# Masked attention stage: score matmuls in four 32-row tiles, one PSUM bank for three uses, and a new order within each batch

## The chip, the cores and the metric

The kernel runs on one NeuronCore of a Trainium2 chip. The metric is the device time of one execution in microseconds (us). The engines are TensorE (PE in the profile, its weight loads PEld), VectorE (DVE), ScalarE (ACT), GpSimd (POOL) and SyncE (SP), each with an instruction stream of its own; they meet at semaphores only. Matmuls write PSUM, which has eight banks of 128 x 512 fp32; VectorE and ScalarE read PSUM, GpSimd reads SBUF only.

## The reference

Four transformer blocks follow one another on `x` (16 batches x 128 rows x 256), each attending to itself or to a context. The change lies in the third block alone, here "the masked stage":

```python
# L2, per layer: self attention with ltor_mask, then cross attention with cross_mask; 16 heads of 16
def attention(q, k, v, mask):
    scores = einsum('bhqd,bhkd->bhqk', q, k) / sqrt(16)
    scores = scores * mask - 10000.0 * (1.0 - mask)
    probs = softmax(scores, axis=-1)
    return einsum('bhqk,bhkd->bhqd', probs, v)
ln_out = layernorm(x); q, k, v = split(ln_out @ w_qkv + b_qkv)          # layer 0
x = x + merge_heads(attention(q, k, v, ltor_mask)) @ w_ao + b_ao
q = layernorm(x) @ w_q + b_q; k, v = split(context @ w_kv + b_kv)        # layer 1
x = x + merge_heads(attention(q, k, v, cross_mask)) @ w_co + b_co
```

Both layers run over 16 batches of 128 queries and 128 keys, so the stage handles 32 batches of one layer each.

## The kernel before

**A window per batch.** `over_sequence` (L397) calls each engine's `window(n, at)` for n = -4 to 34; window n is the one in which batch n of the 32 has its scores ("core"). In the same window `soon` is batch n+1, `ahead` n+2, `past` n-1, `tail` n-2, `late` n-3. Windows 0 to 8 and most others are written out; 9, 10 and 19 to 26 are the bodies of loops. A window has four steps j, one for four heads each (g = 4n + j numbers them). The order of each engine's instructions is the order of the source; nothing is planned at run time. SyncE only loads context rows and masks for this stage.

**A batch's path.** VectorE normalizes the rows (`normalize`, L2295), TensorE turns them and the context rows into `in_bank` (L1349, L1353), ScalarE copies them out scaled as `rows_t` and `cn_t` (L1780, L1791). TensorE projects queries and keys into `project2_bank` (L1376, L1318) and values into `rows_bank` (L1367). VectorE adds the bias to queries and keys (`qk`, L2347) and to values (`vn`, L2329). GpSimd spreads the keys (`spread`, L2766): for one half of the channels (8 heads of 16 rows) it writes `km`, four copies of the keys side by side, each multiplied by a column of 0 and 1 (`head_in_half`) that keeps one head of four.

**Scores.** A head's 16 rows can't be addressed alone, so a matmul contracts 64 rows (four heads) with the spread keys, 4 x 128 columns, and the zeros keep the heads apart. At j = 0 and j = 2 two such matmuls go to the upper and the lower 64 rows of the array and to banks 0 and 1:

```python
for r in range(2):
    half = slice(r * P // 2, (r + 1) * P // 2)
    pe.matmul(score_bank[r][:, :], qk[u][half, j // 2, :], km[u][half, j // 2, :], start=True, stop=True)
```

**Softmax and result.** For each step VectorE multiplies the bank by the mask (L2322), GpSimd adds the mask's bias (L2786), VectorE takes the negative maximum of each head (L2334), ScalarE the exponentials (four instructions, L1752), TensorE turns the four heads' probabilities (`turn_bank`, L1302), ScalarE copies them (L1758), TensorE sums values (L1336, four tiles of 32 columns, one for each head). Once a batch's four sums are done ScalarE copies them (L1762), TensorE turns them back (`unturned_bank`, L1359), VectorE divides by the row sums (L2354, L2094: "heads taken"), TensorE turns the heads (L1309), ScalarE copies them (L1767), TensorE multiplies by the output weights (`rows_bank`, L1325) and VectorE adds to `x` (L2314).

**VectorE's other work.** In each even window at j = 1: one normalization (L2300) and the mean and variance of two later batches (`measure`, `shift`, L2284 to L2292); in each odd window a normalization at j = 3. In windows 0 to 7 also, at j = 1, `standardized` (L2258): two instructions (L2263, L2267) that finish a row of the stage before.

**Banks.** 0 and 1 scores, 2 turned probabilities, 3 sums, 4 projections of queries and keys, 5 turned inputs, 6 sums turned back, 7 in two halves, `rows_bank` and `heads_bank`.

Of the kernel before, what the change touches and what calls it, by code (L numbers as in the profile page):

```python
# [20 lines left out]
F32 = mybir.dt.float32  # L21
# [3 lines left out]
ACT = mybir.ActivationFunctionType  # L25
X_AXIS = mybir.AxisListType.X

P = 128
B = 16
D = 256  # L30
# [462 lines left out]
def program(nc, t, out, outer):  # L493
# [7 lines left out]
    bank = [outer.enter_context(nc.psum_tensor(f"bank{k}", [P, BANK], F32)) for k in range(8)]  # L501
# [56 lines left out]
    with ExitStack() as scope1:  # L558
        head_of_16 = sbuf(scope1, "head_of_16", [P, HN // 2])
        head_in_half = sbuf(scope1, "head_in_half", [P, PACK])  # L560
        vn = [sbuf(scope1, f"vn{u}", [P, UNITS, HN, QUAD]) for u in range(SLOTS)]
# [242 lines left out]
    def _(pe):  # L804
# [473 lines left out]
        def layer2():  # L1278
# [4 lines left out]
            def window(n, at, u=None):  # L1283
                u = n % SLOTS if u is None else u
                core, past, tail, late = at(0), at(-1), at(-2), at(-3)
                soon, ahead = at(1), at(2)
                for j in range(STEPS):
                    g = STEPS * n + j
                    if core and j % 2 == 0:

                        pe.wait_ge(s.spread, 2 * n + j // 2 + 1)
                        after(pe, s.masked, g)
                        for r in range(2):
                            half = slice(r * P // 2, (r + 1) * P // 2)
                            pe.matmul(score_bank[r][:, :], qk[u][half, j // 2, :], km[u][half, j // 2, :], start=True, stop=True)\
                              .then_inc(s.scores, 1)
                    if core and j == 3 or past and j < 3:
                        pe.wait_ge(s.exp_ready, g - 2)
                        after(pe, s.probs_copied, g - 3)
                        t = (j - 3) % STEPS  # L1300
                        for m in range(PACK):
                            last = pe.transpose(turn_bank[:, m * P:(m + 1) * P], probs[t][:, m * P:(m + 1) * P], ident[:, :])  # L1302
                        last.then_inc(s.probs_turned, 1)
                    if late and j == 1:
                        pe.wait_ge(s.heads_taken, n - 2)
                        if core:
                            pe.wait_ge(s.v_ready, n + 1)
                        for c in range(DC):
                            last = pe.transpose(heads_bank[:, c * P:(c + 1) * P], heads_out[0][:, c * P:(c + 1) * P], ident[:, :])  # L1309
                        last.then_inc(s.heads_turned, 1)  # L1310
                    if soon and j == 1:
                        layer, b = soon
                        keys_of = cn_t[1 - u] if layer else rows_t[1 - u]
                        if layer:
                            pe.wait_ge(s.context_ready, b + 1)
                        for m in range(DC, 2 * DC):
                            for c in range(DC):
                                last = pe.matmul(project2_bank[:, m * P:(m + 1) * P], w_qkv[:, layer, c, m * P:(m + 1) * P],  # L1318
                                                 keys_of[:, c, :], start=c == 0, stop=c == DC - 1)
                        last.then_inc(s.projected, 1)  # L1320
                    if late and j == 2:
                        layer = late[0]
                        pe.wait_ge(s.heads_copied, n - 2)
# [4 lines left out]
                        if isinstance(n, int) and n == 2 * B + 1:  # L1328
                            turn_hidden(ROUNDS)
                    for t in (0, 1) if past and j == 1 else (j,) if past and j else ():  # L1330
                        pe.wait_ge(s.probs_copied, g - j + t - 3)
                        if t == 0:
                            pe.wait_ge(s.v_ready, n)
                            after(pe, s.sums_copied, n - 1)
                        for m in range(PACK):
                            last = pe.matmul(sums2_bank[m * QUAD:(m + 1) * QUAD, t * P:(t + 1) * P], vn[1 - u][:, 0, PACK * t + m, :],  # L1336
                                             probs_t[t][:, m * P:(m + 1) * P], start=True, stop=True)
                        last.then_inc(s.sums, 1)
                    if ahead and j == 0:

                        layer, b = ahead
                        if isinstance(n, int) and n == -2:
                            unread(19, sums2_bank)
                        pe.wait_ge(s.rows_normed, n + 3)
                        after(pe, s.in_ready, n + 2)
                        if layer:
                            after(pe, s.context_ready, b)
                        for c in range(DC):
                            last = pe.transpose(in_bank[:, c * P:(c + 1) * P], norm_rows[:, u, c * P:(c + 1) * P], ident[:, :])  # L1349
# [1618 lines left out]
```

## Time and profile before

| | |
|---|---|
| median of 3 runs | 2274.27 us (2271.91 to 2277.16) |
| the profiled execution | 2272.06 us, its span 2270.3 us |
| mean granted TensorE clock | 0.992 |
| masked stage, first scores to the last addition | 1468.8 to 1835.1 us |
| busy in the whole span | PE 2179.0 us (96%), PEld 1779.6, ACT 1573.0 (69%), DVE 1554.7 (68%), POOL 725.4 (32%) |

A busy share is no limit by itself: matmuls are pipelined, so that an engine that is busy nearly all the time may yet wait for operands. What matters for the change is how long one window of the masked stage lasts, and which instruction waits for which in it.

### The profile page before, as it was taken

The page shows a single profiled execution, that of the slowest core. Times are in us where ns is not written, and L with a number is a line of the kernel's source. Part 1 is how long each engine was busy: PE and PEld are TensorE (multiplying, and loading weights), DVE is VectorE, ACT ScalarE, POOL GpSimd, SP SyncE. Part 2 cuts the span into 40 slices and gives each one's busy share as a digit, 9 for nine tenths or more (in the row PEclk, how much of TensorE's full clock was granted, in tenths as well). Part 3 has the DMA queues.
Part 4 walks back from the last instruction along what each step waited for, and adds up shares of the span by engine and source line. Part 5 has one row for each costly group of instructions (what it writes and reads, how often), then busy time and mean ns, then how long its engine had stood idle before and what let it go on. Part 6 is the DMA issues. An engine that isn't in the chain of part 4 may idle for free. (4 is left out here: it accounts for less than half of the span.)

```text
span 2270.3 us, 51859 instructions
## 1 busy us (share of the span) xinstructions
PE 2179.0 (96%) x17621; PEld 1779.6 (78%) x17621; DVE 1554.7 (68%) x3940; ACT 1573.0 (69%) x4479; POOL 725.4 (32%) x885
## 2 busy tenths in 40 slices
PE   8999999999999999998999999889999989999998
PEld 7899999998999999997985666556666679766664
DVE  6555555567555555557759999687776676899985
ACT  4666666665667666665737777577788776578875
POOL 2211111123211111102124655377777720233201
PEclk9999999999999999999989999999999999999999
DMA  5100112010010000002000000100000000000001
GB/s 135 24 25 24 24 25 61 24 24 1 24 24 25 24 24 24 1 1 64 11 8 11 11 9 6 39 8 2 6 15 17 14 8 5 7 11 11 7 4 38
DMA packets 72945, 47.16 MB, mean 21 GB/s; under 512 B 29232, under 2 KB 71600, under 8 KB 72752
## 3 DMA queue, kind: packets, MB, share of 16 engines
q1 hardware_dynamic: 70576, 43.57, 7.3%
q8 instruction: 117, 1.92, 0.3%
q10 hardware_dynamic: 2176, 1.05, 0.2%
q14 instruction: 76, 0.62, 0.1%
HBM read 41.45 MB, written 2.10 MB: 19 GB/s over the span
## 5 line engine op out<-in xcount | busy, mean ns | idle before, releaser
L2155 DVE TENSOR_REDUCE maxima<-bank 128x2 f32<-128x512 f32 x512 | 332.6, 681 | 30.4 <-PE bank L1103 28.3
L1715 ACT ACTIVATE probs_t<-bank 128x512 f32<-128x512 f32 x512 | 282.4, 601 | 64.8 <-PE bank L1092 63.4
L2011 DVE SCALAR_TENSOR_TENSOR wide_heads_low<-bank,wide_columns,wide_heads_high 128x128 fp32r<-128x128 f32 x512 | 155.8, 346 | 209.3 <-ACT wide_heads_high L1580 209.2
L1568 ACT ACTIVATE wide_probs<-bank,wide_neg_max 128x129 f32<-128x129 f32 x512 | 184.2, 365 | 118.7 <-DVE wide_neg_max L1991 114.4
L1563 ACT ACTIVATE wide_probs_t<-bank 128x256 f32<-128x256 f32 x256 | 98.3, 384 | 161.7 <-PE bank L959 159.5
L2512 POOL TENSOR_TENSOR wide_columns<-wide_pair_columns,zero 128x8 f32<-128x8 f32 x16 | 3.3, 209 | 640.7 <-DVE x L2024 638.9
L1995 DVE RECIPROCAL wide_inverse<-wide_sums 128x2 f32<-128x2 f32 x256 | 42.4, 166 | 227.7 <-ACT wide_probs L1568 227.7
L1574 ACT ACTIVATE wide_probs<-wide_probs,wide_inverse 128x128 f32<-128x128 f32 x448 | 156.1, 396 | 52.0 <-DVE wide_inverse L1995 52.0
L1092 PE MATMUL bank<-q_packed,k_packed 32*128 32x256 f32 x1024 | 167.6, 330 | 7.5 <-ACT probs_t L1715 6.8
L1103 PE MATMUL bank<-k_packed,q_packed 32*128 32x256 f32 x1024 | 172.6, 334 | 2.2 <-DVE maxima L2155 1.1
L1752 ACT ACTIVATE probs<-scores_masked,neg_max 128x128 f32<-128x128 f32 x512 | 163.2, 394 | 10.7 <-DVE neg_max L2334 10.0
L973 PEld LDWEIGHTS bank<-wide_probs_t,wide_v 128*128 128x128 f32 x1024 | 148.0, 190 | 26.3 <-ACT wide_probs_t L1563 10.0
L807 PE MATMUL bank<-wide_weights_high,wide_heads_high 128*128 128x256 f32 x512 | 165.6, 323 | 0.2 <-DVE wide_heads_low L2011 0.2
L1092 PEld LDWEIGHTS bank<-q_packed,k_packed 32*128 32x128 f32 x1024 | 104.0, 185 | 74.1 <-ACT probs_t L1715 37.0
L973 PE MATMUL bank<-wide_probs_t,wide_v 128*128 128x128 f32 x1024 | 157.1, 276 | 4.7 <-ACT wide_probs_t L1563 4.7
L946 PE MATMUL bank<-wide_k,wide_q 128*128 128x129 f32 x1024 | 156.0, 275 | 3.0 <-POOL wide_normed_low L2538 1.5
L1580 ACT ACTIVATE wide_heads_high<-bank,wide_columns 128x128 fp32r<-128x128 f32 x512 | 155.2, 353 | 1.5 <-PE bank L973 0.8
L807 PE MATMUL bank<-wide_weights_high,wide_ctx_high 128*128 128x256 f32 x512 | 148.2, 289 | 0.0
L946 PEld LDWEIGHTS bank<-wide_k,wide_q 128*128 128x128 f32 x1024 | 139.9, 190 | 9.6 <-POOL wide_normed_low L2538 2.2
L809 PE MATMUL bank<-wide_weights_high,wide_heads_low 128*128 128x256 f32 x512 | 143.9, 281 | 0.0
L808 PE MATMUL bank<-wide_weights_low,wide_heads_high 128*128 128x256 f32 x512 | 143.9, 281 | 0.0
L808 PE MATMUL bank<-wide_weights_low,wide_ctx_high 128*128 128x256 f32 x512 | 142.9, 279 | 0.0
(319 smaller groups left out, 6799.5 us busy)
## 6 DMA issues: line engine op xcount, KB each, us to landing
cn<-in_ctx SPq DMA_DIRECT2D x48, 128.0 KB, 2.1
q_packed<-max_rows SPq DMA_DIRECT2D x256, 4.0 KB
wide_pair_weights<-in_L_xattn_wq SPq DMA_DIRECT2D x15, 256.0 KB, 2.7
wide_pair_weights<-in_L_xattn_wk SPq DMA_DIRECT2D x15, 256.0 KB, 3.2
wide_pair_weights<-in_L_xattn_wv SPq DMA_DIRECT2D x15, 256.0 KB, 3.5
wide_pair_weights<-in_L_xattn_wo SPq DMA_DIRECT2D x15, 256.0 KB, 3.3
x<-in_x SPq DMA_DIRECT2D x4, 512.0 KB, 7.1
wide_ctx_rows<-in_ctx SPq DMA_DIRECT2D x4, 512.0 KB, 8.7
```

The costliest lines, as they stand in the source:

```text
L807: pe.matmul(acc, wh, mh, start=start, stop=False)
L808: pe.matmul(acc, wh, ml, start=False, stop=False)
L946: last = pe.matmul(wide_scores[b % 2][:, h * KEYS0:(h + 1) * KEYS0], q0[k % 2][:, h, b * P:(b + 1) * P], k0[k % 2][:, h, b, :], start=True ...
L973: last = pe.matmul(wide_heads[a % 2][:, h * P:(h + 1) * P], v0[parity][:, a, h * P:(h + 1) * P], probs_t0[:, a, h, :], start=True, stop=True)
L1092: last = pe.matmul(shifted_bank[j % 2][:, c * D:(c + 1) * D], k_packed[u][quad[a], pack, c * P:(c + 1) * P], q_packed[u][quad[a], pack, :] ...
L1103: last = pe.matmul(head_scores[packed_scores(1 - u, j)][:, c * D:(c + 1) * D], q_packed[1 - u][quad[b], pack, c * P:(c + 1) * P], k_packed ...
L1568: last = act.activation(probs0[:, b, h, :], wide_scores[b % 2][:, h * KEYS0:(h + 1) * KEYS0], ACT.Exp, bias=neg_max0[:, b, h:h + 1], accum ...
L1574: last = act.activation(probs0[:, b, h, 0:P], probs0[:, b, h, 0:P], ACT.Copy, scale=inverse0[:, b, h:h + 1])
L1715: act.activation(probs_t[j % 8][:, :], shifted_bank[j % 2][:, :], ACT.Exp, bias=0.0).then_inc(s.exp_ready, 1)
L1752: last = act.activation(probs[t][:, part], scores_masked[t][:, part], ACT.Exp, bias=neg_max[t][:, h:h + 1])
L2011: last = dve.scalar_tensor_tensor(heads_low[:, h, a, :], wide_heads[a % 2][:, h * P:(h + 1) * P], columns[slot][:, 3, h:h + 1], heads_high ...
L2155: dve.tensor_reduce(maxima[pack // 2][:, b, pack % 2, :], head_scores[packed_scores(1 - u, j)][:, :].rearrange("p (a k) -> p a k", a=UNITS ...
```

## The change

- **Scores.** Four matmuls for each of j = 0 and 2, each on 32 rows of the array (two heads), with 2 x 128 columns of spread keys, into four banks (0 to 3, 256 columns of each). The semaphore is raised after the second and the fourth.
- **Spread keys.** GpSimd writes two copies in place of four: `head_in_quad`, two columns, for `head_in_half`.
- **Mask product** (L2322): reads two half-filled banks in one instruction in place of a full one.
- **Banks.** Turned probabilities go to bank 4, sums to 5; inputs turned, projections, and sums turned back share bank 6, one after the other. The rows and heads bank 7 gets more waits (`heads_copied` ahead of the values and of `vn`).
- **Order.** Inputs of a batch are turned in the window before its scores, no longer two before, and queries and keys are projected together at j = 2. TensorE's window is now (before, the steps j = 0 to 3 were: scores, turn, inputs | turn, heads, keys, two sums, sums back | scores, turn, result, sum | turn, sum, values, queries):

```text
j = 0   scores 0, 1 | turn probs 1 of past | turn inputs of soon
j = 1   result of late | turn probs 2 | sums 0, 1 | sums turned back of tail
j = 2   scores 2, 3 | turn probs 3 | project queries and keys of soon
j = 3   turn probs 0 of core | values of soon | heads of tail | sums 2, 3
```

VectorE adds the bias to queries and keys at j = 3, after the mask product; it takes the heads at j = 2, after the mask product and the maxima of that step, and adds the result to `x` behind them. ScalarE copies the inputs all at j = 0 and the heads at j = 3.

```diff
-    score_bank = [bank[0], bank[1]]
-    turn_bank = bank[2]
-    sums2_bank = bank[3]
-    project2_bank = bank[4]
-    in_bank = bank[5]
-    unturned_bank = bank[6]
+    score_banks = banks[:, 0:PACK, 0:D]
+    turn_bank = bank[4]
+    sums2_bank = bank[5]
+    project2_bank = in_bank = unturned_bank = bank[6]
...
@@ TensorE, window
-                        for r in range(2):
-                            half = slice(r * P // 2, (r + 1) * P // 2)
-                            pe.matmul(score_bank[r][:, :], qk[u][half, j // 2, :], km[u][half, j // 2, :], start=True, stop=True)\
-                              .then_inc(s.scores, 1)
+                        for a in range(PACK):
+                            last = pe.matmul(score_banks[:, a, :], qk[u][quad[a], j // 2, :], km[u][quad[a], j // 2, 0:2 * P], start=True, stop=True)
+                            if a % 2:
+                                last.then_inc(s.scores, 1)
...
+                    if late and j == 1:
+                        layer = late[0]
+                        pe.wait_ge(s.heads_copied, n - 2)
                         if core:
                             pe.wait_ge(s.v_ready, n + 1)
...                                                  # result of late: into rows_bank
+                    if past and j == 1:
+                        turn_probs(g, j)
+                        sum_pair(n, g, j, u)
                     if tail and j == 1:
                         pe.wait_ge(s.sums_copied, n - 1)
                         after(pe, s.heads_taken, n - 2)
+                        if soon:
+                            pe.wait_ge(s.in_ready, n + 2)
+                            if soon[0]:
+                                pe.wait_ge(s.context_ready, soon[1] + 1)
+                        elif core:
+                            pe.wait_ge(s.qk_ready, n + 1)
...                                                  # sums turned back of tail
+                    if soon and j == 2:
+                        layer, b = soon
+                        keys_of = cn_t[1 - u] if layer else rows_t[1 - u]
+                        pe.wait_ge(s.in_ready, n + 2)
+                        if layer:
+                            pe.wait_ge(s.context_ready, b + 1)
+                        if tail:
+                            pe.wait_ge(s.heads_taken, n - 1)
+                        for m in range(2 * DC):
+                            rows = rows_t[1 - u] if m < DC else keys_of
+                            for c in range(DC):
+                                last = pe.matmul(project2_bank[:, m * P:(m + 1) * P], w_qkv[:, layer, c, m * P:(m + 1) * P],
+                                                 rows[:, c, :], start=c == 0, stop=c == DC - 1)
+                        last.then_inc(s.projected, 1)
...
+            def turn_probs(g, j):
+                pe.wait_ge(s.exp_ready, g - 2)
+                after(pe, s.probs_copied, g - 3)
...
+            def sum_pair(n, g, j, u):
+                for t in (0, 1) if j == 1 else (2, 3):
+                    pe.wait_ge(s.probs_copied, g - j + t - 3)
...
@@ VectorE, window
+                        pair = slice(2 * (j % 2), 2 * (j % 2) + 2)
+                        dve.tensor_tensor(scores_masked[j][:, :].rearrange("p (a h k) -> p a h k", a=2, h=2),
+                                          score_banks[:, pair, :].rearrange("p a (h k) -> p a h k", h=2),
+                                          mask[:, 0:1, :].unsqueeze(2).broadcast_to([P, 2, 2, P]), ALU.mult).then_inc(s.masked, 1)
...
+                    if soon and j == 3:
+                        layer = soon[0]
+                        dve.wait_ge(s.projected, n + 2)
...                                                  # qk; then the maxima of the step before
-                    if tail and j == 3:
+                    if tail and j == 2:              # behind the mask product and the maxima of j = 2
                         dve.wait_ge(s.sums_turned, n - 1)
                         after(dve, s.heads_turned, n - 2)
...
@@ GpSimd, spread
-                    pool.tensor_tensor(km[slot][:, c, :].rearrange("p (h k) -> p h k", h=PACK),
-                                       qk[slot][:, DC + c:DC + c + 1, :].broadcast_to(wide),
-                                       head_in_half[:, :].unsqueeze(2).broadcast_to(wide), ALU.mult).then_inc(s.spread, 1)
+                    pool.tensor_tensor(km[slot][:, c, 0:2 * P].rearrange("p (h k) -> p h k", h=2),
+                                       qk[slot][:, DC + c:DC + c + 1, :].broadcast_to(twice),
+                                       head_in_quad.unsqueeze(2).broadcast_to(twice), ALU.mult).then_inc(s.spread, 1)
```

## Rows read from the trace of the kernel before

**Rows 1.** Windows 8, 9: PE, PEld, DVE, ACT, POOL busy; clock, DMA

```profile
1558.66:1580.83 22.17, 21.05 (x177) 14.28 (x177) 16.08 (x33) 17.00 (x49) 16.32 (x16) 1.00 0.01 2
```

**Rows 2.** The score matmuls alone in stretches of whole windows, eight records a window

```profile
1468.80:1490.88 22.08, 5.46 (x16) 1.44 (x16) 0.94 0.00 1
1490.88:1558.66 67.78, 13.55 (x49) 3.62 (x49) 1.00 0.03 7
1558.66:1680.61 121.95, 24.84 (x88) 6.62 (x89) 1.00 0.02 7
1680.61:1769.94 89.33, 18.06 (x64) 4.82 (x64) 1.00 0.06 18
1769.94:1813.40 43.46, 9.03 (x32) 2.41 (x32) 1.00 0.05 14
```

**Rows 3.** Timeline of TensorE, window 10 (start us, us, line, shapes, records)

```profile
1580.83 1.13 PE L1295 MATMUL bank<-km,qk 64*128 64x512 f32 x4
...
1583.33 0.63 PE L1302 MATMUL bank<-ident,probs 128*128 128x128 f32 x4 [0.56 <-ACT probs_t L1758]
...
1585.00 0.64 PE L1336 MATMUL bank<-probs_t,vn 128*32 128x128 f32 x16
1585.57 0.66 PE L1359 MATMUL bank<-ident,sums_copy 128*128 128x128 f32 x4
1586.16 1.13 PE L1295 MATMUL bank<-km,qk 64*128 64x512 f32 x4
...
1589.97 1.13 PE L1367 MATMUL bank<-w_qkv,rows_t 128*128 128x256 f32 x4
1590.93 1.05 PE L1376 MATMUL bank<-rows_t,w_qkv 128*128 128x128 f32 x8
1591.92 0.70 PE L1295 MATMUL bank<-km,qk 64*128 64x512 f32 x2
```

**Rows 4.** Timeline of VectorE, window 10

```profile
1581.99 0.69 DVE L2322 TENSOR_TENSOR scores_masked<-bank,self_mask 128x512 f32<-128x512 f32 x1 [1.33 <-PE bank L1295]
1582.60 0.41 DVE L2329 TENSOR_TENSOR vn<-bank,b_v 128x256 f32<-128x256 f32 x1
1582.93 0.67 DVE L2334 TENSOR_REDUCE neg_max<-scores_masked 128x4 f32<-128x512 f32 x1
...
1584.12 0.67 DVE L2334 TENSOR_REDUCE neg_max<-scores_masked 128x4 f32<-128x512 f32 x1
1584.71 0.99 DVE L2300 TENSOR_SCALAR norm_rows<-x,mean_var,rstd 128x256 f32<-128x256 f32 x1
...
1587.16 0.17 DVE L2292 TENSOR_SCALAR stat_shifted<-mean_var 128x2 f32<-128x2 f32 x1
...
1590.64 0.25 DVE L2354 RECIPROCAL inverse<-bank 128x16 f32<-128x16 f32 x1
1590.92 0.43 DVE L2094 TENSOR_TENSOR heads_out<-bank,inverse 128x256 f32<-128x256 f32 x1
```

**Rows 5.** Timeline of GpSimd, window 10

```profile
1582.76 1.28 POOL L2786 TENSOR_TENSOR scores_masked<-scores_masked,self_mask 128x512 f32<-128x512 f32 x1 [1.21 <-DVE scores_masked L2322]
...
1590.00 1.04 POOL L2768 TENSOR_TENSOR km<-qk,head_in_half 128x512 f32<-128x512 f32 x1
```

**Rows 6.** Timeline of VectorE, windows 2 and 3: first instruction of `standardized`

```profile
1497.29 0.48 DVE L2263 SCALAR_TENSOR_TENSOR x<-x,row_sums,std_t 128x256 f32<-128x256 f32 x1
...
1506.15 0.98 DVE L2263 SCALAR_TENSOR_TENSOR x<-x,row_sums,std_t 128x256 f32<-128x256 f32 x1
```

**Rows 7.** Timeline, window 21, in a loop: scores and their mask product

```profile
1702.94 1.13 PE L1295 MATMUL bank<-km,qk 64*128 64x512 f32 x4
...
1704.28 0.69 DVE L2322 TENSOR_TENSOR scores_masked<-bank,cross_mask 128x512 f32<-128x512 f32 x1 [1.69 <-PE bank L1295]
```

**Rows 8.** Timeline of TensorE in the second stage: 32-row tiles

```profile
1330.65 0.38 PE L1092 MATMUL bank<-q_packed,k_packed 32*128 32x256 f32 x1
...
1330.67 0.38 PE L1092 MATMUL bank<-q_packed,k_packed 32*128 32x256 f32 x1
```

More of the change, by code:

```diff
@@ L498, in sbuf @@
         return scope.enter_context(nc.sbuf_tensor(name, shape, dtype))
-    bank = [outer.enter_context(nc.psum_tensor(f"bank{k}", [P, BANK], F32)) for k in range(8)]
+    banks = outer.enter_context(nc.psum_tensor("banks", [P, 8, BANK], F32))
+    bank = [banks[:, k, :] for k in range(8)]
     x = sbuf(outer, "x", [P, B, D])
@@ new lines, in window @@
+                    if past and j == 0:
+                        turn_probs(g, j)
+                    if soon and j == 0:
+                        layer, b = soon
+                        if isinstance(n, int) and n == -1:
+                            unread(19, sums2_bank)
+                        pe.wait_ge(s.rows_normed, n + 2)
+                        after(pe, s.qk_ready, n + 1)
+                        for c in range(DC):
+                            last = pe.transpose(in_bank[:, c * P:(c + 1) * P], norm_rows[:, 1 - u, c * P:(c + 1) * P], ident[:, :])
+                        if layer:
+                            pe.wait_ge(s.loaded[1 - u], 16 * (b // SLOTS + 1) if isinstance(b, int) else 8 * (b - (1 - u)) + 16)
+                            for c in range(DC):
+                                last = pe.transpose(in_bank[:, (DC + c) * P:(DC + c + 1) * P], cn[1 - u][:, c * P:(c + 1) * P], ident[:, :])
+                        last.then_inc(s.turned, 1)
@@ L1311, in window @@
[L1311 to L1320, printed above, removed]
@@ L1327, in window @@
                         last.then_inc(s.result, 1)
[L1328 to L1349, printed above, removed]
-                        if layer:
-                            pe.wait_ge(s.loaded[u], 16 * (b // SLOTS + 1) if isinstance(b, int) else 8 * (b - u) + 16)
-                            for c in range(DC):
-                                last = pe.transpose(in_bank[:, (DC + c) * P:(DC + c + 1) * P], cn[u][:, c * P:(c + 1) * P], ident[:, :])
-                        last.then_inc(s.turned, 1)
+                    if past and j == 1:
+                        turn_probs(g, j)
+                        sum_pair(n, g, j, u)
                     if tail and j == 1:
@@ L1741, in window @@
                 u = n % SLOTS if u is None else u
-                core, past, tail, late, soon, ahead = at(0), at(-1), at(-2), at(-3), at(1), at(2)
+                core, past, tail, soon = at(0), at(-1), at(-2), at(1)
                 for j in range(STEPS):
```

112 lines of the change are left out of this document (57 added, 55 removed).

## Prediction

> **What bounds the kernel now.** I read the page's table of slices, then how long one window of the masked stage lasts, then one window instruction by instruction. Windows 8 to 18 take 121.95 us for eleven, 11.09 each; in the loops of layer 1 (19 to 26) it is 89.33 / 8 = 11.17 [rows 2]. In windows 8 and 9 TensorE is busy 21.05 of 22.17 us, VectorE 16.08, ScalarE 17.00, GpSimd 16.32 [rows 1]. TensorE looks like the bound, and nearly is: in window 10 one wait of 0.56 us stands before it, at the second turn of probabilities, for ScalarE's copy out of the one bank they share [rows 3]. All else follows back to back. So before, a window is TensorE's work plus 0.56 us, and no engine's long chain is in the way, because what TensorE needs was made a window earlier. The question for the new order is what TensorE needs within the same window.
>
> **Prices.** A record of 256 columns takes 0.215 us: the values, four of them, run from 1589.97 to 1590.93 with 0.11 for the first weight load [rows 3]. One of 128 columns takes 0.11, by the eight of the queries, 0.99 us with the switch to the tiles at their end. So a turn of four is 0.44, the result or the values 0.86 (0.97 after a wait), the projections together 16 x 0.11 + 0.11 = 1.89 (with rounding up of 0.02), the heads 0.22. Going to other tile sizes costs about 0.10. Two sums at once take 0.57, the turning back 0.59, each with the switch behind it [rows 3].
>
> **Scores.** Before, two matmuls of 512 columns run at once, in 1.13 us for both passes. With half the columns each of the two passes is 0.215 shorter, 0.43 in all, if four tiles overlap as two do. In the second stage 32-row tiles of 256 columns start 0.02 us apart (first and third of four) while each takes 0.38 [rows 8]. So I take 0.43 for each pair of steps. VectorE's mask product starts 1.16 us after the scores [rows 3, 4]; now 0.73. Its bounds: 1.16 (nothing saved) and 0.73. The product keeps its 512 elements; from two banks I price it the same, 0.69.
>
> **The spread keys.** 1.04 us for 512 elements [rows 5]; 256 cost between 0.52 and 1.04. I take 0.55. It is cover either way: see below. The extra addition that makes the two columns runs once, far ahead. No DMA is added; the context's load waits for the turned inputs, has two windows for it, and stays off the path.
>
> **The new window, odd n.** I count from the first scores (0).
>
> - The product starts at 0.73, `vn` 0.61 later, takes 0.41, and 0.08 passes to the next engine (product end 1582.68, GpSimd's start 1582.76) [rows 4, 5]: 1.83. The result of `late` waits for `vn`, for it writes the same bank. TensorE, done with scores, a turn and the inputs at about 1.5, stands for 0.3 us.
> - Result 0.97, turn 0.44, switch 0.10, sums 0.57, turning back 0.59: scores 2, 3 start at 4.50. Their banks are free (the second product starts by 2.3, as `vn` and the maxima of the step before take 0.33 and 0.59 [rows 4]). ScalarE, busy 17.00 of 22.17 us [rows 1], should have the inputs out of bank 6 by then, an estimate with about 0.5 us to spare.
> - Now the new wait. The projections write bank 6, where the sums turned back lie until VectorE has taken the heads. VectorE could take them at once, but in its stream the mask product of j = 2 stands ahead, which waits for scores 2, 3. So: 0.73 to the product (5.23), 0.60 for it, 0.59 for the maxima, 0.28 for the reciprocal, 0.43 for the heads, 0.08: 7.21 [rows 4]. TensorE has only a turn to do meanwhile and stands from 5.6 to 7.2.
> - Projections 1.89 (9.10), turn 0.44, values 0.86, heads 0.22, switch 0.10, sums 0.57: the next scores at 11.29. The spread keys they need: bias at about 9.4, 0.68, then 0.55: 10.7; with 1.04 it is 11.2, still in time.
>
> So an odd window takes 11.29, against 11.09. The work itself is only about 9.3: from 10.5 come off 0.86 of scores and, with sums and projections in one piece each, three switches. The two waits, 0.3 and 1.6, eat it.
>
> **Even n.** At j = 1 VectorE has a normalization and two batches' moments before the product of j = 2. They begin 2.72 after the first product (1584.71 - 1581.99), at 3.45, and the last starts 2.45 later [rows 4], 0.08 more until the next can start (my estimate, for so small an operation): the product comes at 5.98 in place of 5.23. Before, this filled a gap; now it stands ahead of the heads, 0.75 us: 12.04. In windows 2, 4, 6 `standardized` adds two instructions of 0.48 and gaps [rows 6]: 1.03, so 13.07. In 3, 5, 7 they are slower (0.98 the first), some 1.9 together, from 3.45 to 5.35 in place of 5.23: 11.41.
>
> **The sum**, with the times before from [rows 2]:
>
> | windows | new | before | |
> |---|---|---|---|
> | 0, 1: no heads to take yet; four pairs of scores 0.43 shorter | 20.4 | 22.08 | -1.7 |
> | 2 to 7 | 3 x (13.07 + 11.41) = 73.4 | 67.78 | +5.7 |
> | 8 to 18 | 6 x 12.04 + 5 x 11.29 = 128.7 | 121.95 | +6.7 |
> | 19 to 26 | 95.1 | 89.33 | +5.8 |
> | 27 to 30 | 4 x 11.29 = 45.2 | 43.46 | +1.7 |
>
> In the loops the product starts 1.34 after the first scores, 0.18 later than elsewhere [rows 7]; I give the second pair half of that: 11.56 and 12.22. In 27 to 30 no moments are left to measure. The last windows I leave as they are: a thin chain with the same links. Total +18.2 us. On the profiled execution's 2272.06 that is 2290.3; the median of the runs is 2.2 above it, so 2292.
>
> **Weighed against the skill.** The mask product that empties the banks costs 0.69 before and after, 0.60 from start to start, and VectorE is busy 16.08 of 22.17 us [rows 1, 4]; so faster scores should bring its start forward in full. The Trainium skill, TensorEngine Tiling (Array Packing), Performance Considerations, says that tiling speeds up the matmuls but not the emptying of PSUM, which may become the bottleneck. By the rows the scores' 0.43 counts wherever the product waits for them; by the rule it would count nowhere, and the sum would be rival 2's.
>
> **Rivals.**
>
> 1. *TensorE's work sets the pace (faster).* For it: it is the busiest engine [rows 1], and its window falls to about 9.3. Then 31 x (11.1 - 9.3) = 56 us less: 2218. It needs the heads taken by 5.6. Against it: the product of j = 2 alone can't begin before 5.23, and the heads follow 1.98 later. Only if VectorE's order didn't bind would it come. 5%. A partial form, in which the waits are shorter by over 0.8 us a window than I make them, gives about 2265: 7%.
> 2. *The shorter scores bring nothing.* Odd windows lose 0.86, even ones 0.43 (there VectorE hides the second pair): 31 x 0.65 = +20, 2312. Against it: VectorE waits 1.33 us for the scores [rows 4]. 5%.
> 3. *The waits let the clock fall.* TensorE stands up to 2.4 us in even windows, 3.4 in early ones. In the first stretch, with its long waits, the granted clock is 0.94, a share of the time at the lower level; elsewhere 1.00 [rows 2]. Were it 0.94 throughout, 6% of 9.3 us x 31 = +17: 2309. 5%.
> 4. *The four tiles don't overlap*: the change doesn't do what it says. Four times 0.43 plus 0.27 is 1.99 where I have 0.70, +1.3 twice in odd windows, once in even: +60, 2352. Against it: rows 8. 3%.
> 5. *No change*: the two waits about 0.6 us a window shorter, since odd windows are only 0.20 above before and a few latencies of 0.1 decide: 2274. 13%.
>
> **How the numbers follow.** My forecast has 62%. Its own range is 2280 to 2306: below, the normalization free of GpSimd (half of its 0.99) and the product nearer to the scores, -0.4 a window; above, the spread keys at 1.04, the later product in every window and the first wait longer, +0.4. To hold 8 in 10 I take in most of case 5 and cases 2 and 3: 2270 to 2312. A measurement here can tell 0.2%, 4.5 us, from no change. Faster 12% (rival 1), same 13% (5), slower 75% (62, 5, 5 and 3).
>
> **What would show it.** Scores at 32 rows x 256 columns taking 0.70 for a pair, and the product 0.73 behind them; TensorE waiting for the heads before the projections, some 1.6 us in odd and 2.4 in even windows, and 0.3 for `vn` before the result; windows of 11.3 and 12.0 in turn. Wrong if the first projection follows the turn of j = 2 at once, or if even and odd windows are alike. The weak points are the latencies, each counted twice in a window, and VectorE's speed while GpSimd works beside it.

## The result, and the profile after

The changed kernel takes 2321.1 us (median of 4 runs, 2320.0 to 2323.8), the kernel before 2274.7 (4 runs): 1.0208 times as long, 95% interval 1.0196 to 1.0220. That is 46 us slower where 18 were forecast, and outside the range. The span of the profiled execution is 2320.3 us, the mean granted clock 0.976 where it was 0.992.

The masked stage first, windows 2 to 30 as one stretch: length, then the busy times of PE, PEld, DVE, ACT and POOL, and the granted clock. The kernel before:

```profile
1490.88:1813.40 322.52, 306.89 (x2569) 208.38 (x2568) 238.88 (x481) 252.24 (x724) 234.43 (x216) 1.00 0.04 11
```

The changed kernel, the same windows, and then windows 12, 13 and 14 one by one:

```profile
1492.06:1861.95 369.89, 301.79 (x2816) 235.28 (x2812) 240.21 (x480) 254.98 (x728) 211.36 (x216) 0.93 0.03 10
...
1624.25:1636.40 12.15, 9.49 (x100) 7.21 (x96) 8.93 (x19) 8.56 (x25) 7.75 (x9) 1.00 0.00 1
1636.40:1647.80 11.40, 9.50 (x101) 7.21 (x97) 7.21 (x14) 8.57 (x25) 6.93 (x8) 1.00 0.01 2
1647.80:1661.31 13.51, 10.88 (x101) 8.59 (x97) 8.93 (x19) 8.57 (x25) 7.75 (x9) 0.87 0.00 1
```

Read the last number but two of each row. Windows 12 and 13 run at full clock and take 12.15 and 11.40 us, where 12.04 and 11.29 were forecast. Window 14 has the work of window 12 and takes 13.51, and its granted clock is 0.87: for a part of it TensorE ran at the lower of its two levels, 1.2 in place of 2.4 GHz. The clock of [rows 2] was 1.00 in every stretch from window 2 on.

Next, TensorE's timeline, in windows 13 and 14 and at the projections of window 12 (it answers to [rows 3]):

```profile
1632.36 2.02 PE L1351 MATMUL banks<-rows_t,w_qkv 128*128 128x128 f32 x16 [2.26 <-DVE heads_out L2108]
...
1636.40 0.71 PE L1293 MATMUL banks<-km,qk 32*128 32x256 f32 x8
1637.05 0.66 PE L1380 MATMUL banks<-ident,probs 128*128 128x128 f32 x4
...
1638.32 1.10 PE L1318 MATMUL banks<-w_out,heads_t 128*128 128x256 f32 x4 [0.40 <-DVE vn L2339]
...
1640.95 0.71 PE L1293 MATMUL banks<-km,qk 32*128 32x256 f32 x8
1641.59 0.66 PE L1380 MATMUL banks<-ident,probs 128*128 128x128 f32 x4
1643.75 2.02 PE L1351 MATMUL banks<-rows_t,w_qkv 128*128 128x128 f32 x16 [1.50 <-DVE heads_out L2108]
...
1647.80 0.71 PE L1293 MATMUL banks<-km,qk 32*128 32x256 f32 x8
...
1655.88 3.40 PE L1351 MATMUL banks<-rows_t,w_qkv 128*128 128x128 f32 x16 [2.24 <-DVE heads_out L2108]
```

The eight records of four 32-row tiles take 0.71 us (0.70 forecast). TensorE stands for the heads, 1.50 us in the odd window and 2.26 in the even one (1.6 and 2.4 forecast), and 0.40 for the biased values (0.3). The last row shows the cost that the sum didn't have: after the stand of 2.24 the same 16 projections take 3.40 us, not 2.02. Window 14 from the start of that stand, cut where its clock changes:

```profile
1653.65:1655.36 1.71, 0.00 (x0) 0.00 (x0) 1.61 (x5) 0.84 (x3) 0.76 (x1) 1.00 0.00 0
1655.36:1658.77 3.41, 2.89 (x13) 2.92 (x14) 1.30 (x3) 1.07 (x4) 1.17 (x2) 0.50 0.00 0
1658.77:1661.31 2.54, 2.54 (x32) 2.02 (x30) 1.28 (x2) 1.07 (x3) 1.22 (x2) 1.00 0.01 3
```

TensorE stands from 1653.65; the clock falls to half at 1655.36, while it still stands, and most of the projections run at the lower level.

VectorE in window 13 (it answers to [rows 4]):

```profile
1637.15 0.69 DVE L2331 TENSOR_TENSOR scores_masked<-banks,self_mask 128x512 f32<-128x512 f32 x1 [1.45 <-PE banks L1293]
...
1641.70 0.69 DVE L2331 TENSOR_TENSOR scores_masked<-banks,self_mask 128x512 f32<-128x512 f32 x1 [1.74 <-PE banks L1293]
1642.31 0.68 DVE L2350 TENSOR_REDUCE neg_max<-scores_masked 128x4 f32<-128x512 f32 x1
1642.90 0.25 DVE L2364 RECIPROCAL inverse<-banks 128x16 f32<-128x16 f32 x1
1643.18 0.42 DVE L2108 TENSOR_TENSOR heads_out<-banks,inverse 128x256 f32<-128x256 f32 x1
```

This is the chain of the forecast: scores 2, 3 at 1640.95, product 0.75 behind them (0.73 forecast), maxima, reciprocal, heads, and at 1643.75 the projections. A spread of keys takes 0.61 to 0.62 us on GpSimd (0.55 forecast; it answers to [rows 5]):

```profile
1624.95 0.62 POOL L2785 TENSOR_TENSOR km<-qk,head_of 128x256 f32<-128x256 f32 x1
```

**Where the 46 us are.** From the first scores of window 0 to those of window 31 it is 391.2 us, before 344.6: +46.6. Fourteen windows of 2 to 30 (2, 5, 6, 8, 9, 10, 14 and 21 to 27) hold time at the lower level. Each is longer than the windows of its kind at full clock, by 1.36 to 1.64 us and once by 2.84; together 23.5. Without that the stage has +23.1, against +18.2 in the table of the forecast. (Windows 0 and 1 are in the +23.1 as they are: their mean clock is 0.83, before 0.94, and what that costs isn't taken out.) In every one of the fourteen the fall begins while TensorE stands for the heads, or at most 0.62 us after. The medians differ by 46, the two profiled executions by 50: in the latter the stage also starts 2.0 later and what follows it takes 1.5 longer (458.4 against 456.9).

### The profile page after: what moved, and what is told of

Read it like the earlier page. It is cut to its first block and busy times, and to the rows that moved or that the text cites. A ratio compares the mean times of both kernels' runs of the same rounds, so it can differ in the third digit from the quotient of the medians.

```text
span 2320.3 us, 52438 instructions
## 1 busy us (share of the span) xinstructions
PE 2178.1 (94%) x17877; PEld 1812.7 (78%) x17877; DVE 1555.1 (67%) x3940; ACT 1572.9 (68%) x4479; POOL 698.6 (30%) x886
## 5 line engine op out<-in xcount | busy, mean ns | idle before, releaser
L2169 DVE TENSOR_REDUCE maxima<-banks 128x2 f32<-128x512 f32 x512 | 332.7, 682 | 31.4 <-PE banks L1103 29.2
L1730 ACT ACTIVATE probs_t<-banks 128x512 f32<-128x512 f32 x512 | 282.4, 601 | 64.1 <-PE banks L1092 62.6
L2025 DVE SCALAR_TENSOR_TENSOR wide_heads_low<-banks,wide_columns,wide_heads_high 128x128 fp32r<-128x128 f32 x512 | 155.9, 346 | 209.0 <-ACT wide_heads_high L1595 208.9
L1583 ACT ACTIVATE wide_probs<-banks,wide_neg_max 128x129 f32<-128x129 f32 x512 | 183.8, 364 | 119.2 <-DVE wide_neg_max L2005 114.6
L1103 PE MATMUL banks<-k_packed,q_packed 32*128 32x256 f32 x1024 | 172.5, 333 | 2.0 <-DVE maxima L2169 1.1
L1092 PE MATMUL banks<-q_packed,k_packed 32*128 32x256 f32 x1024 | 167.2, 330 | 7.1 <-ACT probs_t L1730 6.5
L807 PE MATMUL banks<-wide_weights_high,wide_heads_high 128*128 128x256 f32 x512 | 165.6, 323 | 0.2 <-DVE wide_heads_low L2025 0.2
L973 PE MATMUL banks<-wide_probs_t,wide_v 128*128 128x128 f32 x1024 | 157.1, 276 | 4.5 <-ACT wide_probs_t L1578 4.5
L946 PE MATMUL banks<-wide_k,wide_q 128*128 128x129 f32 x1024 | 156.1, 275 | 3.0 <-POOL wide_normed_low L2554 1.6
L1595 ACT ACTIVATE wide_heads_high<-banks,wide_columns 128x128 fp32r<-128x128 f32 x512 | 155.0, 352 | 1.5 <-PE banks L973 0.8
```

Source lines behind the costliest of these rows:

```text
L807: pe.matmul(acc, wh, mh, start=start, stop=False)
L946: last = pe.matmul(wide_scores[b % 2][:, h * KEYS0:(h + 1) * KEYS0], q0[k % 2][:, h, b * P:(b + 1) * P], k0[k % 2][:, h, b, :], start=True ...
L973: last = pe.matmul(wide_heads[a % 2][:, h * P:(h + 1) * P], v0[parity][:, a, h * P:(h + 1) * P], probs_t0[:, a, h, :], start=True, stop=True)
L1092: last = pe.matmul(shifted_bank[j % 2][:, c * D:(c + 1) * D], k_packed[u][quad[a], pack, c * P:(c + 1) * P], q_packed[u][quad[a], pack, :] ...
L1103: last = pe.matmul(head_scores[packed_scores(1 - u, j)][:, c * D:(c + 1) * D], q_packed[1 - u][quad[b], pack, c * P:(c + 1) * P], k_packed ...
L1583: last = act.activation(probs0[:, b, h, :], wide_scores[b % 2][:, h * KEYS0:(h + 1) * KEYS0], ACT.Exp, bias=neg_max0[:, b, h:h + 1], accum ...
```

## The experiments

My theory: the waits that the new order puts before TensorE cost twice, by their length and because the clock falls over them. Against it stands that they cost their length alone, and the clock's level is chance or belongs to the four tiles. All kernels but the last of these (the kernel before again) are edits of the changed kernel. Times of before on the same chip: 2274.5 for the first move of the heads, the long filler and the two kernels with the old scores; 2274.3 for the short filler, the moments, the wide spread and the kernel before again; 2274.4 for the two with the values first.

**The heads ahead of the mask product of j = 2.** The block that takes the heads moves up in VectorE's window:

```diff
                 for j in range(STEPS):
                     g = STEPS * n + j
+                    if tail and j == 2:
+                        dve.wait_ge(s.sums_turned, n - 1)
+                        ...
+                        weighted(0, heads_out[0][:, :], sums[:, :, 0:16]).then_inc(s.heads_taken, 1)
                     if core:
...
-                    if tail and j == 2:              # the same block, behind the maxima
```

> The changed kernel with one edit: VectorE takes the heads (reciprocal and product) ahead of the mask product of j = 2, not behind the maxima. Theory A (TensorE stands at the projections because VectorE takes the heads behind a mask product that waits for the scores, and it is this standing that lets the granted clock fall): the wait before the projections goes in odd windows (about 9.8 us from scores to scores, where the changed kernel has 11.40) and shrinks to about 1.1 in even ones (10.9 for 12.15), the clock stays at the upper level in the stage, the time is about 2257, faster than before. Rival B (the 32-row tiles or the shared bank cost the time by themselves): windows stay at 11.4 and 12.1, near 2321. Rival C (the clock falls since the scores stream half the columns, whatever the waits): the windows shorten but the clock goes on falling in about a third of them, near 2280.

Measured: 2261.7 us (2261.2 to 2263.0), 0.9944 of before (0.9928 to 0.9961). Odd windows take 9.66 us, even ones 10.94, 9.83 and 11.24 in the loops. The wait for the heads is gone in odd windows and 1.07 in even ones:

```profile
1610.34 1.91 PE L1351 MATMUL banks<-rows_t,w_qkv 128*128 128x128 f32 x15 [1.07 <-DVE heads_out L2108]
```

From window 2 on the clock falls in 4 and 6 alone, where `standardized` makes the wait 2.04 us. A move on VectorE alone thus gives 59 us back, which is more than all that the change cost; 2257 was expected, without any fall. It shortens windows by 1.2 to 1.8 us and mostly keeps TensorE's clock up, so the time by itself doesn't tell which of the two brings the gain. By the windows the two falls cost about 1.6 us each, where the changed kernel loses 23.5: an estimated 20 of the 59 us are the clock, and the rest is shorter waits.

**Throwaway products in the wait.** Between the turn of j = 2 and the projections TensorE does five products of 256 columns in even windows and three in odd ones. They go to the half of the sums' bank that is overwritten later; nothing is left out and no wait is taken away.

```diff
+                        if tail and past:
+                            for k in range(5 if u == 0 else 3):
+                                pe.matmul(sums2_bank[:, 2 * P:4 * P], ident[:, :], w_qkv[:, 0, 0, 0:2 * P], start=True, stop=True)
                         if tail:
                             pe.wait_ge(s.heads_taken, n - 1)
```

> The changed kernel with work added, and nothing else touched: ahead of the projections of j = 2 TensorE multiplies the identity with 256 columns of weights, three times in odd windows (1.3 us) and five times in even ones (2.15 us), into the unused half of the sums' bank, which the sums of j = 3 overwrite later. The additions fit into the wait for the heads (1.5 to 1.6 and 2.3 us). Theory A (the clock falls because TensorE stands there): no fall of the clock in the middle of the stage, every window 11.4 or 12.1 again, some 20 us less than the changed kernel: about 2301, though TensorE does more. Rival C (the clock falls for another reason): as before the addition or later, 2321 or more. Rival D (the falling clock costs nothing, since it falls into waits): 2321.

Measured: 2299.8 us (2295.9 to 2301.3), 1.0106 (1.0087 to 1.0125). TensorE does more work than in the changed kernel and ends 21 us earlier. Odd windows take 11.33 us, even ones 12.07, nearly what they take at full clock without the products (11.40, 12.15), and no window from 2 on has a low clock (2301 was expected). Windows 2 to 30 as one stretch:

```profile
1493.02:1838.40 345.38, 328.98 (x3050) 253.35 (x3046) 240.20 (x480) 255.11 (x728) 211.65 (x216) 1.00 0.04 10
```

The waits for the heads are kept, filled with work, and the loss by the clock is gone. (Only in windows 28 and 30, which have no moments, do five products outlast the wait: 11.81 us.)

**Half as many and fewer: two products in even windows, one in odd.** The same edit with `range(2 if u == 0 else 1)`.

> The changed kernel with less work added to the wait for the heads: one product of 256 columns in odd windows (0.43 us) and two in even ones (0.86), where the earlier run had three and five. If it is the length of TensorE's standing that lets the clock fall, the falls get fewer and don't vanish: between 2300 and 2321, about 2308.

Measured: 2301.3 us (2299.7 to 2301.7), 1.0113 (1.0096 to 1.0130), as good as the long filler, where 2308 was expected. From window 2 on the clock falls in 2 and 6 alone, after stands of 2.59 and 2.27 us; window 4 has one of 2.28 and keeps it. Its windows 7 to 30:

```profile
1558.09:1840.21 282.12, 247.82 (x2412) 187.64 (x2409) 192.76 (x386) 212.63 (x609) 172.91 (x177) 1.00 0.04 11
```

The same windows of the changed kernel:

```profile
1560.78:1861.95 301.17, 249.03 (x2340) 194.08 (x2336) 192.77 (x386) 212.47 (x609) 172.56 (x177) 0.94 0.04 10
```

VectorE, ScalarE and GpSimd are busy for the same time in both; TensorE has 72 more records and the stretch is 19 us shorter, at a clock of 1.00 against 0.94. TensorE still stands 0.98 us in an odd and 1.28 in an even window:

```profile
1647.85 2.05 PE L1354 MATMUL banks<-rows_t,w_qkv 128*128 128x128 f32 x16 [1.28 <-DVE heads_out L2111]
```

So with stands of 0.98 and 1.28 us (1.06 and 1.45 in the loops) the clock stayed up in all of these 24 windows, and with 1.50 and 2.26 it fell in 11 of them. The products shorten the stand, come ahead of it and add work all at once; these runs don't part the three.

**The old scores in the new order.** Two 64-row tiles of 512 columns into two banks, spread keys four copies wide; all the rest is the changed kernel.

```diff
-                        for a in range(PACK):
-                            last = pe.matmul(score_banks[:, a, :], qk[u][quad[a], j // 2, :], km[u][quad[a], j // 2, 0:2 * P], start=True, stop=True)
-                            if a % 2:
-                                last.then_inc(s.scores, 1)
+                        for r in range(2):
+                            half = slice(r * P // 2, (r + 1) * P // 2)
+                            pe.matmul(score_bank[r][:, :], qk[u][half, j // 2, :], km[u][half, j // 2, :], start=True, stop=True)\
+                              .then_inc(s.scores, 1)
```

> The changed kernel, its order and its shared bank kept, with the scores as before: two matmuls of 64 rows and 512 columns into banks 0 and 1, the keys spread four wide, the mask product on one full bank. Theory A: the product comes 0.43 us later behind each pair of scores, twice on the path of an odd window and once on that of an even one: 12.26 and 12.6 at full clock, 20 us in all. If the falls of the clock stay as they are: 2341. Rival C (few streamed columns in the scores let the clock fall): the falls go, 2341 - 23 = 2318. Rival B (32-row tiles cost time by themselves): faster than 2321 with windows under 11.4.

Measured: 2334.8 us (2333.0 to 2336.9), 1.0265 (1.0248 to 1.0282). Its windows at full clock take 12.22 and 12.55 us, against 11.40 and 12.15: the four tiles are worth 0.82 in an odd and 0.40 in an even window (0.86 and 0.43 forecast) and 14 us in the whole; that is less than the windows at full clock give (16 x 0.82 + 13 x 0.40 = 18; 28 and 30, without moments, count as odd), since this kernel has fewer windows with a low clock, which is also why it is 6 under the 2341 expected. The spread keys are wide here too, but VectorE doesn't wait for GpSimd in even window 14, so the 0.40 is the scores'. The clock falls here too (in nine even windows, 14.19 where 12.55 is full clock), so it doesn't belong to the four tiles.

**The old scores in the new order, and a bank of its own for the sums turned back.** With two score banks one of the others is free. The waits of the projections for the heads, and of the turned sums for the inputs, fall away with the bank that they protected.

```diff
-    project2_bank = in_bank = unturned_bank = bank[6]
+    project2_bank = in_bank = bank[6]
+    unturned_bank = bank[2]
```

> The kernel with the scores as before in the new order, and the bank so freed (bank 2) given to the sums turned back; the waits that guarded the shared bank (the projections for the heads taken, the turning back for the inputs copied out) are not needed and not there. Theory A: TensorE no longer stands before the projections, windows of about 10.7 (odd) and 11.0 (even, by VectorE's chain to the spread keys), the clock stays up, about 2266, 75 us under the same kernel with the shared bank. Rival B (the order of the steps costs, not the bank): near the same kernel with the shared bank, 2320 to 2340.

Measured: 2277.2 us (10 runs, 2271.6 to 2280.3), 1.0008 (0.9996 to 1.0019). Windows of 10.73 and 11.05 us (11.15 and 11.55 in the loops), and no low clock from window 2 on. Beside the kernel with the old scores and the shared bank that is 58 us less: the shared bank is what the waits come from. It is 11 slower than expected. In its trace, from window 8 on, TensorE still waits 0.39 to 0.56 us for the wide spread keys (in even windows, in the loops in all) and 0.40 for the biased values; what they cost together wasn't tried in this kernel.

**The heads first, and the moments of later batches at j = 2.** The first edit, and `measure`, `measure`, `shift` behind the heads and the addition to `x`:

```diff
-                    if not u and at(4) and j == 1:
+                    if not u and at(4) and j == 2:     # now behind the addition to x
                         measure(n + 4, at(4)[1], 0)
                         measure(n + 5, at(5)[1], 1)
                         shift(n + 4)
```

> The changed kernel with VectorE's heads ahead of the mask product of j = 2, as in the first run, and the even windows' means and variances (measure, shift) moved from j = 1 to j = 2, behind the addition to x. Theory A: TensorE waits for the heads in no window; odd ones stay at 9.66, even ones fall from 10.94 to about 10.4, where VectorE's own work up to the bias of queries and keys is next; some 7 us under the first run, 2255. Rival: GpSimd's power of the variance, now later, delays the spread keys and takes the gain back: 2262.

Measured: 2250.0 us (2247.6 to 2256.3), 0.9886 (0.9870 to 0.9903). Even windows fall from 10.94 to 10.51, odd ones stay at 9.66 (2255 was expected). From window 8 on no wait for the heads is left. Another has come, at the start of an odd window:

```profile
1590.30 0.71 PE L1293 MATMUL banks<-km,qk 32*128 32x256 f32 x8 [0.78 <-POOL km L2785]
```

**The values first as well.** The bias of the values ahead of the mask product of j = 0, on top of both.

```diff
+                    if core and j == 0:
+                        dve.wait_ge(s.values, n + 1)
+                        ...
+                        dve.tensor_tensor(vn[u][:, 0, :, 0:16], rows_bank...).then_inc(s.v_ready, 1)
                     if core:                           # mask product
...
-                    if core and j == 0:                # the same block, behind it
```

> The kernel of the run before it with both other moves (heads ahead, moments last), and one more: VectorE adds the bias of the values ahead of the mask product of j = 0 instead of behind it. In the changed kernel TensorE stands 0.40 us in front of the result of j = 1, 3 because the biased values come late. My theory: that 0.40 us, and some of ScalarE's copy behind it, goes: odd windows from 9.66 to about 9.2 us, even ones from 10.51 to about 10.1, in all about 13 us less than that kernel's 2250, so 2237. Rival: the result waits for ScalarE's copy of the masked scores or the mask product now comes that much later, and the gain is eaten: 2248 to 2252. Nothing is left out of the computation.

Measured: 2238.9 us (2236.4 to 2243.6), 0.9839 (0.9823 to 0.9856): faster than both kernels, by 36 and 82 us. Windows 13 and 14, and the first scores of window 15:

```profile
1604.02 0.71 PE L1293 MATMUL banks<-km,qk 32*128 32x256 f32 x7
1604.66 0.66 PE L1380 MATMUL banks<-ident,probs 128*128 128x128 f32 x4
1605.16 0.38 PE L1306 MATMUL banks<-ident,norm_rows 128*128 128x128 f32 x2
1605.37 1.03 PE L1318 MATMUL banks<-w_out,heads_t 128*128 128x256 f32 x4
...
1608.93 0.63 PE L1380 MATMUL banks<-ident,probs 128*128 128x128 f32 x4 [0.28 <-ACT probs_t L1773]
1609.39 1.95 PE L1351 MATMUL banks<-rows_t,w_qkv 128*128 128x128 f32 x16
...
1613.37 0.71 PE L1293 MATMUL banks<-km,qk 32*128 32x256 f32 x8
...
1623.28 0.71 PE L1293 MATMUL banks<-km,qk 32*128 32x256 f32 x8 [0.50 <-POOL km L2785]
```

The result follows the inputs at once, the projections the turn. The odd window is 9.35 us, of which TensorE stands 0.28 for ScalarE's copy; without that it is 9.07, and the forecast put TensorE's work at about 9.3. The even one is 9.92, and ends on the spread keys. So the work that the change takes off TensorE is real; its windows 2 to 30 say how much:

```profile
1490.59:1782.02 291.43, 268.09 (x2817) 210.49 (x2813) 241.35 (x480) 252.99 (x728) 210.78 (x216) 1.00 0.04 12
```

TensorE is busy 268.1 us, before 306.9, both at a clock of 1.00: 38.8 less, 1.34 a window.

**The values first, alone.** That last move by itself in the changed kernel, where the wait for the heads stays.

> The changed kernel with that one move alone: the bias of the values ahead of the mask product of j = 0. The wait of 1.5 and 2.3 us for the heads stays. My theory: an odd window of 11.40 becomes about 11.0 and an even one of 12.15 about 11.8, some 12 us over the stage, and the granted clock still falls in about as many windows: 2309. Rival: the heads wait swallows it (TensorE is earlier at the projections and stands longer there), and nothing comes of it: 2321. Nothing is left out of the computation.

Measured: 2310.8 us (2309.4 to 2311.9), 1.0157 (1.0140 to 1.0174). At full clock odd windows take 10.76 us (9, 11, 13) and 10.98 (15, 17), where the changed kernel has 11.40; the one even window of this kind at full clock, 16, takes 11.90 for 12.13. 2309 was expected. The clock still falls, in twelve windows of 2 to 30, now all even, in four of them for twice as long. The stands for the heads are 2.04 to 2.30 us in even windows from 8 on and 1.12 to 1.18 in odd ones. The mean clock of the stretch is 0.92:

```profile
1492.99:1852.40 359.41, 297.02 (x2816) 234.22 (x2812) 241.15 (x480) 253.91 (x728) 210.34 (x216) 0.92 0.03 10
```

**Spread keys as wide as before.** GpSimd writes four copies, and the scores read the first two.

```diff
-                    pool.tensor_tensor(km[slot][:, c, 0:2 * P].rearrange("p (h k) -> p h k", h=2),
-                                       qk[slot][:, DC + c:DC + c + 1, :].broadcast_to(twice),
-                                       head_in_quad.unsqueeze(2).broadcast_to(twice), ALU.mult).then_inc(s.spread, 1)
+                    pool.tensor_tensor(km[slot][:, c, :].rearrange("p (h k) -> p h k", h=PACK),
+                                       qk[slot][:, DC + c:DC + c + 1, :].broadcast_to(wide),
+                                       head_of_16[:, 0:PACK].unsqueeze(2).broadcast_to(wide), ALU.mult).then_inc(s.spread, 1)
```

> The changed kernel with the keys spread four wide again (1.04 for 0.61 us on GpSimd, twice in a window); TensorE reads the first two copies as before. By my prediction the narrower spread hides at the scores (in time even at 1.04). What I left out: GpSimd's queue behind it. The bias of the mask for step 3 and the second spread then come later, the first mask's bias of the window starts at about 2.1 in place of 1.5, and the maxima in front of the even window's normalization by 0.6. So odd windows stay at 11.40, even ones go from 12.15 to about 12.7: +8, 2329. If the whole is cover: 2321.

Measured: 2324.7 us (2323.5 to 2325.1), 1.0217 (1.0200 to 1.0234), 3.6 above the changed kernel's median; intervals that overlap. Odd windows at full clock stay at 11.39 us, even ones take 12.39 for 12.15; 2329 and 12.7 were expected. VectorE in even window 14, whose first scores start at 1654.38:

```profile
1657.75 0.69 DVE L2350 TENSOR_REDUCE neg_max<-scores_masked 128x4 f32<-128x512 f32 x1 [0.41 <-POOL scores_masked L2803]
...
1660.67 0.69 DVE L2331 TENSOR_TENSOR scores_masked<-banks,self_mask 128x512 f32<-128x512 f32 x1
```

GpSimd's second spread of 1.04 us lies ahead of its first mask bias of the window, so the second bias ends late and VectorE's maxima wait 0.41 us for it. The normalization and the moments follow, and the product of j = 2 comes 6.29 us behind the first scores, 6.05 in the changed kernel. In an odd window VectorE's gap before scores 2, 3 takes the delay in.

**The kernel before again**, once, with a profile, to see how much of a start 2 us later belongs to the change.

> The kernel before, unchanged, for a second trace: is the masked stage's start (1468.8) and the clock ahead of it the same from run to run? If the clock's falls ahead of the stage shift with the run, the start lies near 1470.7 as in the changed kernel; if not, 1468.8 again, and the 2 us by which the changed kernel comes later have another cause.

Measured: 2276.4 us; its stage starts at 1473.2 us, before at 1468.8, the changed kernel's at 1470.8. The clock in the last 11 us ahead of the stage is 0.70 here; in the trace of before it is 0.97 there, in that of the changed kernel 0.72. The start moves by more than the changed kernel's 2.0 us from one execution of the same kernel to another, so the later start needn't be an effect of the change. Its windows of 11.09 and 11.17 us repeat.

## Why the prediction was right in sign and wrong in size

- **The tiles, the product, the spread keys: right.** 0.71 us for a pair of steps, the product 0.75 behind it where 1.16 was, and it reads two banks in the same 0.69. In the four-tile kernel against its twin with the old scores windows differ by 0.82 and 0.40, as the sum had it. So the scores' time counts wherever the product waits for them, as the rows had it, and the rule that was weighed against them (the Trainium skill, TensorEngine Tiling (Array Packing), Performance Considerations) doesn't decide here. Rival 2 gave 2312 with no gain from the tiles; with none it is 2335.
- **The new window: right, a little short.** Odd 11.40 for 11.29, even 12.15 for 12.04, with `standardized` 13.13 and 11.61 for 13.07 and 11.41, in the loops 11.67 and 12.53 for 11.56 and 12.22. Together with windows 0 and 1 (21.26 for 20.4) that is +23.1 in place of +18.2. The loops are the largest part, 1.7 of the 4.9: even windows there are 0.31 longer than forecast, odd ones 0.11.
- **"It is cover either way": half right.** With 1.04 us the odd window stays, the even one grows by 0.24; GpSimd's mask biases stand behind the spread, and the step looked at TensorE alone. And the cover is gone once the other waits are: in the faster versions the spread keys are what TensorE waits for, 0.78 and 0.50 us.
- **The step that failed: the waits were priced by their length alone.** The sum puts what the clock does over them at nothing. The mechanism stood beside it as rival 3, "the waits let the clock fall", with 5%, and the case for so little was weak: one average of 0.94 over two windows, and a clock of 1.00 in windows where TensorE never stood longer than 0.78 us (0.56 in the row that was read), which says nothing of stands of 1.5 and more. The trace shows the fall in 14 of 29 windows, 23.5 us; two fillers, of 3 or 5 and of 1 or 2 products, lift the clock and give 21 and 20 us back with the heads as late as before and work added. The forecast of 2292, with 23.5 for the clock and the 4.9 by which the waits were short, comes to 2320, where 2321.1 was measured. Rival 3's own figure, 2292 + 17 = 2309, has the right form, the clock on top of the waits, and is short by the same 4.9 and by 6.5 of the clock's price.
- **The Trainium skill tells of such a loss** in another kernel, in TensorE: Matmul & The Clock Gate, A second HAM failure mode: psum-queue depth-cycling: short idle stretches between groups of matmuls, come often enough, make the clock go back and forth. This case's trace agrees: stands of 1.50 and 2.26 us in windows of 11.40 and 12.15, and a granted clock of 0.93 over 370 us.
- **Rival 1 needed one more move.** It said that the window would fall to TensorE's work, 2218, if VectorE's order didn't bind. With three blocks of VectorE moved the windows are 9.35 and 9.92 and the time 2239. The change was held back by the place of two blocks in VectorE's stream, and by the moments in even windows.

**Open.** Which windows have the low clock. Windows 11 to 13 have the instructions of 8 to 10, and 19 and 20 those of 21 to 26, and keep the full clock. So do 15 to 18, in which TensorE turns the context's rows as well (and stands 0.18 us before the result in place of 0.40), though it stands 2.23 us before the projections in the even ones. With one more small edit other windows have the low clock. No run here tells why a stand of the same length brings a fall in one window and not in another.

## What to carry to other kernels

When two uses of a bank are put one behind the other, look in the stream of the engine that empties it for what stands ahead of the emptying, and move the emptying first: here a block moved up by two instructions was worth 59 us, more than the 38.8 us of matmul work that the change saved in the stage. Where a forecast has TensorE standing in each round about as long as here (1.5 and 2.3 us of 11.4 and 12.15), add the price of the lower clock to the sum, from a row that has it, as a term with a chance, not as a rival. And a few throwaway matmuls in a wait that can't be removed are a cheap test of that price; here they also cured it.

## What the runs showed of the hardware that was not expected

- Every fall between windows 2 and 30, 51 in the six traces that have any, begins while TensorE stands for the heads or at most 1.4 us after that stand. None follows a stand under 1.50 us (0.98 to 1.45 beside the short filler, 1.12 to 1.18 in the odd windows with the values first), while some stands of 2.2 to 2.5 us, and one of 3.24, have none behind them.
- One throwaway product of 256 columns in an odd window and two in an even one, 0.43 and 0.86 us of work, did as much as three and five: 2301.3 and 2299.8 us.
- Windows with throwaway products are 0.07 to 0.08 us shorter than windows of the same kind at full clock without them (11.33 for 11.40, 12.07 for 12.15).
- Taking 0.40 us of a stand away in front of the result did not lift the clock while the one for the heads stayed: 0.92 in windows 2 to 30, where it was 0.93.
